# Light attention scores as three rounded products, with a new order of the projections around them

## The reference: what is computed

```
x = x + 0.5 * ffn(layernorm(x))      # 8 experts of width 128, the top 2 per token
x = x + attn(layernorm(x))
x = x + 0.5 * ffn(layernorm(x))      # the same weights again
```

```
z        = layernorm(y) * ln_g + ln_b
q, k, v  = split(z @ wqkv_l)                  # 8 heads of 64
light    = softmax(q k' / 8) v @ wo_l         # windows of 64 tokens; each sees itself and both neighbours
heavy    = softmax attention of 256 queries over 256 keys, picked by two routing scores (y . rt_q, y . rt_kv),
           added back to the tokens that it was computed for
```

## Time and profile before

| | |
|---|---|
| median of 3 runs | 2155.14 us (2154.74 to 2159.65) |
| the profiled execution | 2159.13 us, span 2157.3 us |
| TensorE matmuls busy | 2032.7 us, 94% |
| weight loads busy | 1586.8 us, 74% |
| DVE busy | 1581.0 us, 73% |
| ACT busy | 1243.2 us, 58% |
| POOL busy | 1036.4 us, 48% |
| granted TensorE clock, mean | 0.983 |
| scores of the first item / of the last one start | 494.0 us / 1686.8 us |

### The profile page before, as it was taken

How to read it: one execution, slowest core, us unless ns; L and a number is a source line. 1 busy time by engine, 2 the same in 40 slices (tenths; PEclk the granted TensorE clock), 3 DMA queues, 4 the chain that set the end, 5 groups by cost and what they waited for, 6 DMA issues and landing times.

```text
span 2157.3 us, 40188 instructions
## 1 busy us (share of the span) xinstructions
PE 2032.7 (94%) x13232; PEld 1586.8 (74%) x13232; DVE 1581.0 (73%) x5207; ACT 1243.2 (58%) x2948; POOL 1036.4 (48%) x1150
## 2 busy tenths in 40 slices
PE   5999999989999999998998998998999799999998
PEld 5888888876666666666666666666666588888887
DVE  5888888988576677576575675675664388888887
ACT  5555555556656557657557556566555355555554
POOL 3444444545536447347247256265353344444444
PEclk9999999999999999999999999999999799999999
DMA  6111111000111011011011021020010401111110
GB/s 231 60 60 40 40 40 40 30 20 18 33 52 31 13 57 33 6 64 31 1 65 30 1 66 29 3 70 23 18 47 12 134 30 39 38 37 37 39 40 30
DMA packets 72326, 91.19 MB, mean 42 GB/s; under 512 B 6432, under 2 KB 66232, under 8 KB 71096
## 3 DMA queue, kind: packets, MB, share of 16 engines
q1 hardware_dynamic: 61368, 69.39, 9.6%
q0 software_dynamic: 8448, 18.95, 3.0%
q10 hardware_dynamic: 2304, 0.28, 0.1%
HBM read 40.23 MB, written 48.37 MB: 41 GB/s over the span
## 4 chain that ended last, share of the span: by engine, by line
PE 57%; DVE 20%; issue 10%; POOL 8%; ACT 4%; DMA 0%; DVEq 0%; POOLq 0%; ACTq 0%
PE bank L501 10%; PE bank L503 9%; PE bank L502 9%; PE bank L707 5%; PE bank L696 5%; PE bank L667 4%; PE bank L678 4%; PE bank L639 3%; PE bank L528 3%; DVE st L996 3%; DVE xb L1084 2%; POOL tri L1297 2%; POOL hl L1328 2%; DVE wt L1056 2%; DVE scj L1146 2%
## 5 line engine op out<-in xcount | busy, mean ns | idle before, releaser
L1367 POOL TENSOR_TENSOR prob<-prob,rden 128x512 f32<-128x512 f32 x320 | 335.9, 1051 | 548.4 <-DVE rden L1221 546.2
L1084 DVE SCALAR_TENSOR_TENSOR xb<-bank,gate,xb 128x256 f32<-128x256 f32 x1024 | 423.5, 476 | 94.2 <-PE bank L503 93.1
L1328 POOL TENSOR_TENSOR hl<-hf,hh 128x512 fp32r<-128x512 f32 x256 | 330.4, 1298 | 226.2 <-ACT hh L794 216.3
L921 ACT ACTIVATE prob<-prob,nmax 128x256 f32<-128x256 f32 x512 | 256.2, 503 | 282.8 <-DVE nmax L1203 281.1
L793 ACT ACTIVATE hf<-bank,b1s 128x512 f32<-128x512 f32 x256 | 176.3, 689 | 335.9 <-PE bank L503 327.9
L1203 DVE CUSTOM_DVE_ANT_0 prob<-bank,mask 128x256 f32<-128x256 f32 x512 | 195.3, 418 | 149.5 <-PE bank L667 148.3
L501 PE MATMUL bank<-w_hi,hh 128*128 128x256 f32 x1024 | 294.7, 288 | 6.2 <-POOL hl L1328 4.0
L502 PE MATMUL bank<-w_hi,hl 128*128 128x256 f32 x1024 | 289.2, 282 | 0.0
L503 PE MATMUL bank<-w_lo,hh 128*128 128x256 f32 x1024 | 289.1, 282 | 0.0
L501 PE MATMUL bank<-xt_hi,w_hi 128*128 128x512 f32 x512 | 215.2, 420 | 8.4 <-DVE w_lo L1123 8.3
L501 PEld LDWEIGHTS bank<-w_hi,hh 128*128 128x128 f32 x1024 | 194.3, 190 | 29.0 <-POOL hl L1328 18.7
(11 more groups left out here) (165 smaller groups left out, 4403.3 us busy)
## 6 DMA issues: line engine op xcount, KB each, us to landing
xb<-in_L_attn_x SPq DMA_DIRECT2D x16, 512.0 KB, 3.8
x_d<-xb SPq DMA_DIRECT2D x16, 512.0 KB, 2.9
x<-x_d SPq DMA_DIRECT2D x8, 1024.0 KB, 5.6
x_d<-x SPq DMA_DIRECT2D x8, 1024.0 KB, 4.4
xb<-x_d SPq DMA_DIRECT2D x16, 512.0 KB, 3.9
out<-xb SPq DMA_DIRECT2D x16, 512.0 KB, 2.9
hrow<-hs_d SPq DMA_DIRECT2D x16, 257.0 KB, 2.7
w_d<-w_hi SPq DMA_DIRECT2D x2, 1024.0 KB
```

Of the source, the lines that this page charges most:

```text
L921: act.activation(prob[j % NP][:, h, :], src, ACT.Exp, bias=nmax[:, j % 4, h:h + 1], scale=-1.0 if light else 1.0, accum_out=den[:, j % 4, ...
L1084: dve.scalar_tensor_tensor(out=x, in0=bank[ob][:, (t % 2) * D:(t % 2 + 1) * D], scalar=gate[:, k % 2, t, e:e + 1], in1=x, op0=ALU.mult, op ...
L1328: pool.tensor_tensor(hl[i % NH][:, :], hf[i % NH][:, :], hh[i % NH][:, :].bitcast(F32), ALU.subtract).then_inc(s_hl)
L1367: pool.tensor_tensor(prob[j % NP][:, :, :], prob[j % NP][:, :, :], rden[:, j % 4, :].unsqueeze(2).broadcast_to([P, 2, KEYS]), ALU.mult).th ...
```

## The change

**Scores.** q and k are kept in two parts. ACT writes the upper part out of PSUM as float32r, and DVE then subtracts it from the same bank and writes the lower part (two new kinds of DVE instruction, 16 a row). `scores` of a light item becomes six float32r matmuls instead of two float32 ones: q_hi k_hi, q_hi k_lo, q_lo k_hi, each for both heads in turn before the next. It waits for both banks before the first. A q or k bank is left when DVE's part is done (`s_qklo`).

**Room.** q is kept for half a row (512 tokens), v in 6 places instead of 9, and `srow` (routing scores of one router), `z_row` (half a row), `hin` and `xf_t` once instead of twice. The halo of both k parts is cleared (four memsets instead of two).

**Order.** The projections have new slots: in a row's own slots 0 to 18 stand 10 instead of 12, q of the second half row in slots 13 to 16; the second two of the `z` turns of the next row move from slots 17 and 19 to 19 and 21, `z` of its second half row from slots 11 and 12 to 15 and 16, the rows of routing scores for keys from slot 20 to 34, and its rank pieces are in two lots (slots 21 to 33 and 35 to the next row's 6). For row 0 some of these stand a slot or more later.

```diff
-        QKV_AT = (on(-20, 2, 1, 2), on(-14, 2, 1, 2), on(-8, 2, 1, 2, 1), on(0, 1, 2, 1), on(6, 1, 1, 2), on(11, 1, 2, 1))
+        QKV = ((-19, 1, 0, 0), (-18, 1, 0, 1), (-17, 2, 0, 0), (-16, 1, 0, 2), (-15, 1, 0, 3), (-14, 2, 0, 1), (-12, 2, 0, 2),
+               (-11, 0, 0, 0), (-10, 0, 0, 1), (-9, 0, 0, 2), (-8, 0, 0, 3), (-6, 2, 0, 3), (-5, 1, 1, 0), (-3, 2, 1, 4),
+               (-2, 1, 1, 1), (1, 1, 1, 2), (3, 1, 1, 3), (5, 2, 1, 5), (9, 2, 1, 6), (12, 2, 1, 7),
+               (13, 0, 1, 0), (14, 0, 1, 1), (15, 0, 1, 2), (16, 0, 1, 3), (18, 2, 1, 8))   # slot, q/k/v, half, number
...
-            return SLOTS * b + (-28, -26, -23, -21)[i]          # zt_slot
+            return SLOTS * b + (-28, -26, -21, -19)[i]
...
-            return SLOTS * b - 31 + q // 2                      # z_slot
+            return SLOTS * b - (31 if q < TG else 27) + q // 2
...
-            return SLOTS * b - 21 + i // 2                      # srow_slot
+            return SLOTS * b + (-21, 3 if b == 0 else -6)[i // 2]
...
-                return i - 10 if i < 10 else (i - 10) // 2      # rank_slot
-            return SLOTS * b - 19 + i * 26 // 32
+                return i - 10 if i < 10 else (i - 10) // 2 + (i >= 16)
+            return SLOTS * b + (-19 + i * 13 // 16 if i < 16 else -5 + (i - 16) * 12 // 16)
...
             if kind == "qkv":
-                return s_qkv, 25 * x + i + 1
+                if QKV[i][1] == 2:
+                    return s_v, (T + 1) * x + QKV[i][3] + 1
+                return s_qklo, 16 * x + qk_before(i) + 1
...
-                    hs = slice(h * DH, (h + 1) * DH)
-                    if t < T:
-                        ins = pe.matmul(bank[g % NS][:, 0:KEYS], qT[hs, hp, t * P:(t + 1) * P], kT[hs, hp, t * P:t * P + KEYS], start=True, stop=True)
...
+                hs = [slice(h * DH, (h + 1) * DH) for h in range(2)]
+                into = [bank[(2 * j + h) % NS][:, 0:KEYS] for h in range(2)]
+                if t < T:
+                    q0 = t % TG * P
+                    for p, (qn, kn) in enumerate(((0, 0), (0, 1), (1, 0))):
+                        for h in range(2):
+                            ins = pe.matmul(into[h], qT[qn][hs[h], hp, q0:q0 + P], kT[kn][hs[h], hp, t * P:t * P + KEYS], start=(p == 0), stop=(p == 2))
+                            if p == 2:
+                                ins.then_inc(s_sim)
...
                     if kk == 0:
-                        ins = act.activation(qT[:, n, g * NG:(g + 1) * NG], pv[:, :], ACT.Copy, scale=DH ** -0.5)
+                        act.activation(qT[0][:, n, :], pv[:, :], ACT.Copy, scale=DH ** -0.5).then_inc(s_qkhi)
                     elif kk == 1:
-                        ins = act.activation(kT[:, n, HALO + g * NG:HALO + (g + 1) * NG], pv[:, :], ACT.Copy)
+                        act.activation(kT[0][:, n, HALO + g * NG:HALO + (g + 1) * NG], pv[:, :], ACT.Copy).then_inc(s_qkhi)
...
+                if kind == "qkv" and QKV[i][1] < 2:             # DVE's evac, between turned and reciprocals
+                    _, kk, g, n = QKV[i]
+                    dve.wait_ge(s_qkhi, 16 * x + qk_before(i) + 1)
+                    if kk == 0:
+                        ins = dve.scalar_tensor_tensor(out=qT[1][:, n, :], in0=pv[:, :], scalar=DH ** -0.5, in1=qT[0][:, n, :].bitcast(F32),
+                                                       op0=ALU.mult, op1=ALU.subtract)
+                    else:
+                        cols = slice(HALO + g * NG, HALO + (g + 1) * NG)
+                        ins = dve.tensor_tensor(kT[1][:, n, cols], pv[:, :], kT[0][:, n, cols].bitcast(F32), ALU.subtract)
+                    ins.then_inc(s_qklo)
```

More of the change, by code:

```diff
@@ L148, in build @@
         oT_s = sb("oT_s", [P, HC, P])
-        hin_off = room(2 * C * NSEL * 4)
-        hin = [at(f"hin{r}", [P, C, NSEL], F32, hin_off + r * C * NSEL * 4) for r in range(2)]
+        hin = sb("hin", [P, C, NSEL])
         hq = sb("hq", [P, HC, NSEL])
@@ L161, in build @@
         ho = sb("ho", [P, ST, D])
-        xf_off = room(2 * C * 2 * P * 4)
-        xf_t = [at(f"xf_t{i}", [P, C, 2 * P], F32, xf_off + i * C * 2 * P * 4) for i in range(2)]
+        xf_t = sb("xf_t", [P, C, 2 * P])
         top[0] = z2
@@ L243, in due, with qk_before, v_at @@
             return [(b, i) for b in range(ROWS) for i in range(count) if slot_of(b, i) == u]
-        def on(first, *steps):
-            return tuple(itertools.accumulate(steps, initial=first))
-        QKV_AT = (on(-20, 2, 1, 2), on(-14, 2, 1, 2), on(-8, 2, 1, 2, 1), on(0, 1, 2, 1), on(6, 1, 1, 2), on(11, 1, 2, 1))
-        QKV_AT = tuple(itertools.chain(*QKV_AT))
+        QKV = ((-19, 1, 0, 0), (-18, 1, 0, 1), (-17, 2, 0, 0), (-16, 1, 0, 2), (-15, 1, 0, 3), (-14, 2, 0, 1), (-12, 2, 0, 2),
[3 rows of a table added]
+        assert len(QKV) == 3 * HC * 2 + 1 and all(x < y for x, y in zip(QKV, QKV[1:]))
+        def qk_before(i):
+            return sum(q[1] < 2 for q in QKV[:i])
+        def v_at(b, t):
+            return (b * (T + 1) + t) % NV
         def qkv_slot(b, i):
-            return SLOTS * b + QKV_AT[i]
+            return SLOTS * b + QKV[i][0]
         def zt_slot(b, i):
-            return SLOTS * b + (-28, -26, -23, -21)[i]
+            return SLOTS * b + (-28, -26, -21, -19)[i]
         def stat1_slot(b, q):
@@ L638, in heavy_project @@
                         for c in range(C):
-                            ins = pe.matmul(bank[tb][:, j * NSEL:(j + 1) * NSEL], w[:, c, ch * P:(ch + 1) * P], hin[r][:, c, :],
+                            ins = pe.matmul(bank[tb][:, j * NSEL:(j + 1) * NSEL], w[:, c, ch * P:(ch + 1) * P], hin[:, c, :],
                                             start=(c == 0), stop=(c == C - 1))
@@ L642, in heavy_project @@
                     for c in range(C):
-                        ins = pe.matmul(bank[tb][:, :], hin[1][:, c, (i - 4) * P:(i - 3) * P], wkvh_s[:, c, INNER:2 * INNER],
+                        ins = pe.matmul(bank[tb][:, :], hin[:, c, (i - 4) * P:(i - 3) * P], wkvh_s[:, c, INNER:2 * INNER],
                                         start=(c == 0), stop=(c == C - 1))
@@ L664, in scores @@
                             pe.wait_ge(s_nm, g - NS + 1)
-                    hs = slice(h * DH, (h + 1) * DH)
-                    if t < T:
-                        ins = pe.matmul(bank[g % NS][:, 0:KEYS], qT[hs, hp, t * P:(t + 1) * P], kT[hs, hp, t * P:t * P + KEYS], start=True, stop=True)
-                    else:
-                        ins = pe.matmul(bank[g % NS][:, 0:KEYS], hq[hs, hp, (t - T) * P:(t - T + 1) * P], hk[hs, hp, :], start=True, stop=True)
-                    ins.then_inc(s_sim)
+                hs = [slice(h * DH, (h + 1) * DH) for h in range(2)]
[8 more added lines that the diff above has]
+                else:
+                    for h in range(2):
+                        pe.matmul(into[h], hq[hs[h], hp, (t - T) * P:(t - T + 1) * P], hk[hs[h], hp, :], start=True, stop=True).then_inc(s_sim)
             def turn(j):
@@ L1411, in pool_program @@
             pool.wait_ge(s_wst, 16 * 5)
-            pool.memset(kT[:, :, 0:HALO], 0.0).then_inc(s_halo)
-            pool.memset(kT[:, :, HALO + N:PADDED], 0.0).then_inc(s_halo)
+            for part in kT:
+                pool.memset(part[:, :, 0:HALO].bitcast(F32), 0.0).then_inc(s_halo)
+                pool.memset(part[:, :, HALO + N:PADDED].bitcast(F32), 0.0).then_inc(s_halo)
             for u in slots():
```

107 lines of the change are left out of this document (51 added, 56 removed).

## The result

The changed kernel takes 2231.74 us (median of 4 runs, 2225.65 to 2232.09), the kernel before 2157.39 us (4 runs) beside it: 1.0333 times as long, 95% interval 1.0317 to 1.0349 (the ratio is taken over the single runs and is not the quotient of the two medians). The forecast was 2167, with a range up to 2212. The direction was right and the time lies 20 us outside the range. The profiled execution has a span of 2223.9 us, 66.6 more than the one before.

What follows compares the result with a forecast made beforehand. TensorE was taken to bind only slots 16 to 34, POOL 8 to 15, DVE's chain 35 to 7. Six rows +12, start and row 0 +3, row 7 -3: +12, so 2167 us (own range 2160 to 2182; eight in ten 2130 to 2212).

Steps and rivals of the forecast that it cites:

- slots 8 to 15: First stretch of a batch row: POOL's unchanged list, 27.45 us starting 2.4 late, sets 29.8 us, against 31.8 before.
- slots 16 to 34: Middle stretch of a row: TensorE work 76.1 us plus 2.5 of waits, 78.6 us, against 76.5 before.
- slots 35 to 7: Last stretch, into the next row: DVE's late maxima hold back scores, 45.9 us, against 45.3 before.
- the clock: TensorE at half clock after idle gaps in slots 36, 39, 4 and 11: 1.5 us a row more.
- the start and row 0: Two more projections ahead of the first scores (2.8 us), rank pieces still doubled up: +3 us.
- three signs of being wrong: Slots 35 to 7 under 43 us, slots 8 to 15 under 29, or a score pair outside 0.52 to 0.58.
- The score pair: Light scores on TensorE: three steps with heads side by side, 0.555 us, 0.077 less, worth its price only in slots 16 to 34.
- The rival of serial heads: Scores' heads run one after another, 0.91 us a pair, about 2230 us in all; chance 0.10.
- The lower parts: 128 DVE subtractions: 88 us busy, 11 a row, about 0.62 each, plus standing for ACT in five slots a row.
- bare odd slot: Odd slot without an out_proj that DVE evacuates (1, 3, 15, 31, 35): DVE stands 1.4 us for ACT, then works 0.62.
- The z stall: Slots 11-12: ACT waits 2.77 us for POOL's norm, V is late, out_proj waits 2.54; claimed to go.
- The rival "banks and clock": TensorE waits 0.4 to 1 us for q and k banks in neighbouring job slots, half clock behind: 2195 us; chance 0.15.

Runs made afterwards that it cites:

- experiment 5: POOL's two indirect adds of the heavy rows moved to slots 16 and 19: 0.992 of before on the kernel before, 1.0235 on the changed kernel.
- experiments 3 and 6: Changed kernel with DVE's emptying at the end of the slot: 1.0226 of before; also with ACT's first projection emptied earlier and POOL's adds moved: 1.0212.
- busy-time run: Changed kernel with DVE's 128 subtractions made from SBUF to SBUF, waiting for nothing and nobody waiting for them: 2193.53 us, 1.0162 of before.

## Why the prediction was wrong, step by step

The forecast gave the profiled execution +12 us; it got +66.6. Of the 54.6 between them, slots 8 to 15 have 25, slots 16 to 34 11 and slots 35 to 7 5 in six rows, from which the 9 forecast apart for the clock come off; the start and row 0 have 23, the end -2 (what is left is rounding and the part of a row that the three stretches miss). Of my three signs of being wrong none appeared: each stretch sign asked only whether it was too short.

**The score pair** was right: 0.55 us, with three common steps. So was its reading: worth its price in the middle stretch alone (1.2 us a row there in the old slots, 1.3 in the new). The rival of serial heads named 2230, the measured number, by a mechanism that the runs exclude.

**The lower parts.** Right: 0.69 each, at least 1.36 us of standing in every bare odd slot (1.4 forecast), the chain by `maxima` to the scores. Wrong: their number. Row 3 has DVE standing ahead of 14 of the 16, not of five: 1.36 or more in all odd slots, and 0.36 to 0.76 in five even ones, where `turned` was to cover it. In slots 24 to 31 this costs nothing, since TensorE's work fills them; elsewhere it does. By differences of the runs the lower parts make a full row 8.6 us longer (161.6 against 153.0), 5.6 of it in slots 35 to 7, 2.2 in 16 to 34, 0.5 in 8 to 15 (these three by starts of rows 1 to 6, the last stretch reaching into row 7). The 45.9 forecast for 35 to 7 came near 46.7 partly by luck: without lower parts the new slots need 41.1 there, 3.9 less than the old.

**Slots 8 to 15, the first step that failed** (29.8 forecast, 34.0 measured: 4.2 a row, 25 us in six). That POOL binds it is shown by experiment 5, and it is not the lower parts: without them the stretch takes 33.5. I set the length of POOL's list equal to its busy time, 27.45. But in the earlier trace rows the same list filled 32.65, and only 2.0 of that was a wait for DVE; the other 3.2 are gaps between dependent instructions and ahead of its DMAs. Its length without that wait is 30.6. And the list was not unchanged. POOL's timeline at the start of the stretch, after:

```profile
1021.06 0.24 POOL L1314 TENSOR_SCALAR tri<-mv 128x4 f32<-128x4 f32 x1 [5.45 <-issue]
...
1022.84 2.04 POOL L1387 TENSOR_TENSOR prob<-prob,rden 128x512 f32<-128x512 f32 x2
1025.47 1.04 POOL L1387 TENSOR_TENSOR prob<-prob,rden 128x512 f32<-128x512 f32 x1 [0.60 <-DVE rden L1230]
```

A half-row norm (L1314 to L1320), which began 2.2 us ahead of slot 8 before, at 976.96, starts after an idle time of POOL of 5.45 us and falls into the stretch, as in all of rows 1 to 6: 1.8 more. The profile names no releaser for it; in both traces it starts some 0.15 us after ACT has written `y_row` (L832, L822 before). With 0.6 of waiting that is 33 of the 34. The z stall is gone as forecast (15.2 us of TensorE's waits for V ahead of `out_proj` before, none after), and it paid nothing, since POOL, not V, was next in line: 32 us of waits for `prob` where there were 4.

**Slots 16 to 34** (78.6 forecast, 80.5 measured, 11 us in six rows). Without lower parts they take 78.4: the count of work was right. The other 2.2 us are mostly longer slots 16 and 17 (1.2 in the mean of rows 1 to 6), where the scores wait for `maxima`, and slot 23 (0.7), where a projection waits 1.1 us for the bank that a `kT_lo` holds, against 0.35 for ACT without lower parts. I had priced such losses with the single slot 31, which is no longer at all.

**The start and row 0, the second step that failed** (+3 forecast, +26.3 measured). The run with old scores and no lower parts has 13.8 of it, that with three products 15.3, so slots and buffers make some 14 and lower parts 11. In the run with old scores the first scores come 5.5 later, of which I had counted 2.8 for two projections. In the changed kernel the first projection itself starts 2 later (475.40 against 473.35): ACT stands 5.70 for POOL's `xt_lo` (1.69 before) before it writes `z` of the second half row. That the single `xf_t` and the half-row z buffer make it stand is argued from the program, not tried. In row 0 the scores wait longer for `maxima`; which of the moved pieces does it was not tried and stays open.

**The clock.** Windows of rows 1 to 6, after and then without lower parts:

```profile
668.27:1638.11 969.84, 867.98 (x6084) 642.65 (x6085) 680.47 (x2509) 574.70 (x1627) 462.66 (x529) 0.96 0.10 32
```

```profile
657.25:1575.32 918.07, 855.36 (x6084) 632.98 (x6085) 619.94 (x2413) 574.56 (x1627) 461.65 (x529) 0.98 0.11 34
```

The granted clock is 0.96 against 0.98, TensorE busy 12.6 us longer with the same matmuls: 2.1 us a row, where I had 1.5. TensorE's idle time grows by 39.2. Most of the 2.1 lies in one place. Slots 4 and 5 of row 3, after and then without lower parts:

```profile
1005.36:1010.20 4.84, 1.87 (x21) 1.31 (x19) 3.58 (x15) 2.22 (x8) 1.35 (x3) 0.84 0.27 85
1010.20:1017.52 7.32, 7.32 (x33) 5.65 (x33) 6.39 (x27) 3.58 (x12) 3.41 (x5) 0.64 0.00 0
```

```profile
973.47:976.38 2.91, 1.79 (x20) 1.27 (x19) 2.88 (x13) 2.33 (x8) 1.45 (x3) 1.00 0.26 77
976.38:981.26 4.88, 4.88 (x34) 3.78 (x33) 4.88 (x20) 1.95 (x9) 2.88 (x5) 1.00 0.12 38
```

In slot 4 TensorE is idle for 2.97 of 4.84 us, 1.87 of it at the end, for `maxima`; in slot 5 it waits for nothing and yet takes 7.32 us for 4.88, at 0.64 granted. All of rows 1 to 6 have this: slot 5 takes 7.0 in the mean for 4.9. So of the 5.6 us that the lower parts cost in slots 35 to 7, 2.1 are the clock behind one wait. The half level (1.2 GHz) comes back with the waits; that it only multiplies them and has no cause of its own is argued from these lines, not tested alone. The rival "banks and clock" took the banks for the source. The changed kernel waits 13 us for them in all; they matter more when the lower part is moved back (experiments 3 and 6).

The range failed because serial heads were its only large loss, and it left those out; the sum for slots 8 to 15 took a queue's busy time for its length, and no rival priced that. The page "Perfetto Trace Analysis" of the Trainium skill, section "Identifying the Most-Contended Engine", says to optimize the engine with the highest occupancy first, and to judge TensorE by MFU and weight loads rather than by matmul busy time. By matmuls (94%) and, barely, by weight loads (74%, DVE 73%) that was TensorE. The traces agree by half: 9 of 20 us in one run, 38 of 80 in another; the move that by itself beat the kernel before was on POOL, the least busy engine.

## What to carry to other kernels

Take the length of a queue's stretch from first start to last end, less its waits for other engines; busy time leaves out the gaps between dependent instructions. A new instruction that waits for another engine costs its duration and its standing separately: look what stands ahead of its producer (here the exponentials ahead of ACT's copy), for moving the producer up gave more than moving the consumer back. A long queue on the least busy engine can bind a stretch that its share of the span hides.

## What the runs showed of the hardware

Matmuls of two heads on different halves of the partitions run side by side even when the program issues all of one head first: starts in pairs 10 ns apart, 0.55 us for both, as issued by turns. And an idle guard can be dear: a wait on DVE that protects nothing cost 27 us. On DVE's and POOL's common use of SBUF: the 128 lower parts with one input in PSUM took 680 to 693 ns, all of them; the same instruction from SBUF to SBUF 677 to 2228 (busy-time run). The Trainium skill's "SBUF — State Buffer", section "Who interferes with whom", says that only the second kind contends with GpSimd, when that reads SBUF. The traces agree: 20 of the 128 from SBUF to SBUF took over 800 ns, each of them while POOL was computing (17 times beside `xt_lo`), where 21 of the lower parts from PSUM met a POOL operation (16 times `xt_lo`) and none was longer for it.
